# Attention scores: three single PSUM banks in a ring in place of pairs, with one exponential for each bank

## The reference, cut to what matters

```python
qkv = xf @ w_qkv + b_qkv                       # q, k, v: (b, heads, t, 32), t = 1024
scores = jnp.einsum('bhqd,bhkd->bhqk', q, k) * 32 ** -0.5
attn = jax.nn.softmax(scores, axis=-1)
o = jnp.einsum('bhqk,bhkd->bhqd', attn, v)     # then a projection and the residual
```

## Time and profile before

| | us |
|---|---|
| median of 3 runs | 5707.2 (5702.43 to 5717.48) |
| the profiled execution | 5702.98 |
| its span | 5701.3 |

### The profile page before, as it was taken

The page is one execution under the profiler, slowest core; times in us unless marked ns, Lnnn a source line. Parts: engine busy times, 40 slices in busy tenths (PEclk is TensorE's granted clock), DMA queues, the critical chain, the costliest instruction groups (busy, mean ns, idle before and its releaser), DMA issues.

```text
span 5701.3 us, 44537 instructions
## 1 busy us (share of the span) xinstructions
PE 4237.7 (74%) x16298; PEld 1839.3 (32%) x16298; DVE 3892.5 (68%) x4825; ACT 2109.0 (37%) x2575; POOL 2221.3 (39%) x721
## 2 busy tenths in 40 slices
PE   4678866788658886588865878658786587855878
PEld 2233422333224332243322433223332243322433
DVE  7764788647886478764787646876468774686746
ACT  3233442334423344233442435324253242542424
POOL 4541435414454044540445404444045440454404
PEclk7689977899778997699977999769897798976999
DMA  0020100211002100021000220002200012000120
GB/s 34 0 52 16 30 8 4 49 24 22 8 8 45 33 13 8 8 45 36 10 8 8 45 45 1 8 9 44 45 1 8 18 35 45 8 1 18 27 45 8
DMA packets 58845, 125.24 MB, mean 22 GB/s; under 512 B 14713, under 2 KB 16889, under 8 KB 58370
## 3 DMA queue, kind: packets, MB, share of 16 engines
q1 hardware_dynamic: 58626, 122.39, 9.2%
HBM read 12.23 MB, written 8.39 MB: 4 GB/s over the span
## 4 chain that ended last, share of the span: by engine, by line
PE 44%; DVE 34%; issue 9%; ACT 5%; SPq 4%; POOL 2%; DMA 2%; DVEq 0%; ACTq 0%; POOLq 0%
DVE mx L947 10%; PE PS L1288 8%; PE PS L1246 7%; PE PS L1080 6%; PE PS L1336 6%; PE PS L1370 4%; DVE work L839 3%; PE PS L1139 2%; DVE work L841 2%; PE PS L1180 2%; DVE mboth L954 2%; SPq L284 2%; PE PS L1297 2%; DVE small L714 2%; SPq L293 1%
## 5 line engine op out<-in xcount | busy, mean ns | idle before, releaser
L947 DVE TENSOR_REDUCE mx<-PS 128x1 f32<-128x512 f32 x2048 | 1336.3, 686 | 419.5 <-PE PS L1246 415.2
L617 ACT ACTIVATE PT<-PS 128x1024 f32<-128x1024 f32 x1024 | 1007.4, 1022 | 706.5 <-PE PS L1336 679.1
L1246 PE MATMUL PS<-KS,QS 96*128 96x512 f32 x2048 | 894.7, 479 | 194.6 <-DMA KS<-piece 84.6
L423 POOL TENSOR_TENSOR piece<-PT 128x2048 f32<-128x2048 f32 x48 | 219.9, 4581 | 2000.2 <-ACT PT L617 2000.2
L423 POOL TENSOR_TENSOR piece<-piece,PT 128x2048 f32<-128x2048 f32 x192 | 877.4, 4570 | 61.7 <-ACT PT L617 50.4
L399 POOL TENSOR_TENSOR work<-work,Crep 128x1024 f32<-128x1024 f32 x256 | 615.7, 2406 | 434.2 <-DVE work L839 240.9
L1336 PE MATMUL PS<-QS,KS 98*128 98x512 f32 x2048 | 685.2, 427 | 50.3 <-DMA QS<-nm 32.2
L1246 PEld LDWEIGHTS PS<-KS,QS 96*128 96x128 f32 x2048 | 376.7, 197 | 814.9 <-DVE mx L947 575.1
L1288 PE MATMUL PS<-PT,Vt 128*32 128x512 f32 x4096 | 554.1, 613 | 7.6 <-ACT PT L617 7.6
L1180 PE MATMUL PS<-dstk,sel 128*128 128x512 f32 (+1 forms) x640 | 313.1, 564 | 320.6 <-DVE work L841 133.5
L1180 PE MATMUL PS<-ustk,sel 128*128 128x512 f32 (+1 forms) x640 | 329.4, 587 | 285.4 <-DVE work L824 155.0
(11 more groups left out here) (212 smaller groups left out, 5556.3 us busy)
## 6 DMA issues: line engine op xcount, KB each, us to landing
QS<-piece SPq DMA_DIRECT2D x384, 128.0 KB, 2.4
KS<-piece SPq DMA_DIRECT2D x384, 128.0 KB, 2.4
xin<-x SPq DMA_DIRECT2D x8, 1024.0 KB
out<-xr SPq DMA_DIRECT2D x8, 1024.0 KB, 4.0
W<-wpack SPq DMA_DIRECT2D x2, 1024.0 KB
QS<-nm SPq DMA_DIRECT2D x128, 8.0 KB, 1.9
W<-wpack SPq DMA_DIRECT2D x1, 576.0 KB
W<-wpack SPq DMA_DIRECT2D x2, 256.0 KB
```

The costliest lines, as they stand in the source:

```text
L423: pool.tensor_tensor(total, first, PT[:, i % 3, :, :], ALU.add).then_inc(sum_pool.sem, 1)
L617: act.activation(PT[:, i % 3, 2 * pr:2 * pr + 2, :], PS[:, 2 + 2 * pr:4 + 2 * pr, :], ACT.Exp, scale=SCALE).then_inc(p_sb.sem, 1)
L947: dve.tensor_reduce(mx[:, cc, at:at + 1], PS[:, row_slot(n, cc), :], AX.X, ALU.max).then_inc(r_max.sem, 1)
L1246: pe.matmul(PS[:, row_slot(n, cc), :], QS[0:kd, c, h, q * P:q * P + P], KS[0:kd, h, cc * N:cc * N + N], start=True, stop=True).then_inc(r_ ...
```

## The change

The scores of the four heads go in turn through banks 2, 3 and 4 (`score_slot`), and each bank has an exponential of its own over 512 columns: twice as many (2048 in place of 1024), of half the width. A score waits for the exponential three scores earlier. The row scores go in turn through banks 5, 6 and 7, and one waits for the maximum three row scores earlier; in the prologue nothing changes but how the same wait is written. The second row score of a step is issued behind score 2 in place of behind score 3. Semaphore counts follow (`p_sb` and `s_ps` count single scores; the values, POOL's and DVE's additions wait for all four of a step, as before). The transpose of the turn still goes to bank 6.

```diff
@@ -53,6 +53,7 @@
 TURN_AT = 7
 AHEAD = 3
 NORM_AT = 4
+RING = 3
 PHASE_ROWS = sum(HALF_ROWS) // NC
 
 POOL_SUMS = (0, 1, 2, 3, 5, 6)
@@ -238,7 +239,7 @@
         nm_in = sig("nm_in", 2 * PHASES * 2 * 16)
         sum_pool = sig("sum_pool", 2 * (PHASES - 1) * (len(POOL_SUMS) - 1))
         sum_dve = sig("sum_dve", 2 * (len(DVE_SUMS) - 1))
-        s_ps, p_sb = sig("s_ps", 128), sig("p_sb", 128)
+        s_ps, p_sb = sig("s_ps", 256), sig("p_sb", 256)
         pv_ps, den_ln, den_rc = sig("pv_ps", 64), sig("den_ln", 8), sig("den_rc", 8)
         o_raw, o_sb = sig("o_raw", 8), sig("o_sb", 8)
 
@@ -419,7 +420,7 @@
                             first = PT[:, key_step(a, ph, 0) % 3, :, :] if k == 1 else total
                             if k > 1:
                                 pool.wait_ge(*sum_pool(b, pool_sums(a, ph, k - 1)))
-                            pool.wait_ge(*p_sb(b, 2 * i + 2))
+                            pool.wait_ge(*p_sb(b, GH * i + GH))
                             pool.tensor_tensor(total, first, PT[:, i % 3, :, :], ALU.add).then_inc(sum_pool.sem, 1)
                 pool.wait_ge(*x_new(b, 16))
 
@@ -612,9 +613,9 @@
                             done = summed(a, *divmod(i % (PHASES * KT) - 3, KT))
                             if done:
                                 act.wait_ge(*(sum_pool, sum_dve)[done[0]](b, done[1]))
-                        for pr in range(2):
-                            act.wait_ge(*s_ps(b, 2 * i + pr + 1))
-                            act.activation(PT[:, i % 3, 2 * pr:2 * pr + 2, :], PS[:, 2 + 2 * pr:4 + 2 * pr, :],
+                        for j in range(GH):
+                            act.wait_ge(*s_ps(b, GH * i + j + 1))
+                            act.activation(PT[:, i % 3, j, :], PS[:, score_slot(i % (PHASES * KT), j), :],
                                            ACT.Exp, scale=SCALE).then_inc(p_sb.sem, 1)
                         if kt == TURN_AT and ph < PHASES - 1:
                             neg_max(ph + 1)
@@ -995,7 +996,7 @@
                     first = PT[:, key_step(a, ph, 0) % 3, :, :] if k == 1 else total
                     if k > 1:
                         dve.wait_ge(*sum_dve(b, dve_sums(a, k - 1)))
-                    dve.wait_ge(*p_sb(b, 2 * i + 2))
+                    dve.wait_ge(*p_sb(b, GH * i + GH))
                     dve.tensor_tensor(total, first, PT[:, i % 3, :, :], ALU.add).then_inc(sum_dve.sem, 1)
                 normalize(ph)
 
@@ -1240,9 +1241,9 @@
                     if c == 0 and q == 0 and cc == 0:
                         pe.wait_ge(*stackedq[g][j](b, (a + 1) * 48))
                         pe.wait_ge(*stackedk[g][j](b, (a + 1) * 48))
-                    ahead = 2 if ph == 0 else 1
-                    if n % PHASE_ROWS >= ahead:
-                        pe.wait_ge(*r_max(b, halves(a, n - ahead, cc) + 1))
+                    ahead = 2 * NC if ph == 0 else RING
+                    if NC * (n % PHASE_ROWS) + cc >= ahead:
+                        pe.wait_ge(*r_max(b, halves(a, n, cc) - ahead + 1))
                     pe.matmul(PS[:, row_slot(n, cc), :], QS[0:kd, c, h, q * P:q * P + P], KS[0:kd, h, cc * N:cc * N + N],
                               start=True, stop=True).then_inc(r_ps.sem, 1)
 
@@ -1280,7 +1281,7 @@
                     g = ph // NC
                     sums = POOL_SUMS if ph < PHASES - 1 else DVE_SUMS
                     direct = [k for k in range(KT) if k not in sums]
-                    pe.wait_ge(*p_sb(b, 2 * i + 2))
+                    pe.wait_ge(*p_sb(b, GH * i + GH))
                     if kt == 0 and ph > 0:
                         pe.wait_ge(*o_raw(b, i // KT))
                     for j in range(GH):
@@ -1328,15 +1329,13 @@
                             else:
                                 next_rows(NC)
                             pe.wait_ge(*nm_in(b, 32 * (PHASES * a + ph + 1)))
-                        for pr in range(2):
-                            if ph + kt > 0:
-                                pe.wait_ge(*p_sb(b, 2 * i - 2 + pr + 1))
-                            for jj in range(2):
-                                h = GH * g + 2 * pr + jj
-                                ins = pe.matmul(PS[:, 2 + 2 * pr + jj, :], KS[:, h, kt * P:kt * P + P], QS[:, c, h, :],
-                                                start=True, stop=True)
-                            ins.then_inc(s_ps.sem, 1)
-                            next_rows(1)
+                        for j in range(GH):
+                            if GH * (KT * ph + kt) + j >= RING:
+                                pe.wait_ge(*p_sb(b, GH * i + j - RING + 1))
+                            pe.matmul(PS[:, score_slot(i % (PHASES * KT), j), :], KS[:, GH * g + j, kt * P:kt * P + P],
+                                      QS[:, c, GH * g + j, :], start=True, stop=True).then_inc(s_ps.sem, 1)
+                            if j in (1, 2):
+                                next_rows(1)
                         if kt > 0:
                             values(i - 1, next_rows, ph + 1 if kt == TURN_AT and ph < PHASES - 1 else None)
                         next_rows(row[1])
@@ -1402,7 +1401,12 @@
 
 def row_slot(n, cc):
 
-    return (4 + 2 * (n % 2) if n < PHASE_ROWS else 6) + cc
+    return 4 + 2 * (n % 2) + cc if n < PHASE_ROWS else 5 + (NC * (n % PHASE_ROWS) + cc) % RING
+
+
+def score_slot(i, j):
+
+    return 2 + (GH * i + j) % RING
 
 
 def halves(a, n, cc):
```

## The result

| | us |
|---|---|
| before, median of 5 runs | 5707.20 (5700.89 to 5717.95) |
| after, median of 5 runs | 5730.98 (5724.78 to 5735.08) |
| ratio after / before | 1.0037, 95% interval 1.002 to 1.0054 |
| the profiled execution of after, and its span | 5724.78, 5723.0 |

The changed kernel is slower by 24 us between the medians, and by 5723.0 - 5701.3 = 21.7 us between the two profiled spans. The forecast was +63. In the profiled executions the mean granted clock fell from 0.848 to 0.842.

A forecast was written before the change was run, and what follows sets the result against it. It took POOL's chain of five additions, then the turn through `mboth`, transpose and scores, to set each phase's pace. Terms -50 + 12 - 3 + 48 + 56 = +63 us on 5702.98 gave 5766 us, range just under 5710 to 5830.

The forecast's parts named there:

- POOL's gap: The wait ahead of POOL's fourth addition goes as row scores over three banks bring steps sooner: -50 us.
- Eight single exponentials: ACT's eight take 4.24 us, not 3.85: +12 us in phases 1 and 2, -3 us in phase 0.
- Phase 3: Three score banks make a closed round in phase 3: 2.74 us a step against 2.25, +48 us.
- The turn and the clock: PE stands longer before the transpose, TensorE's clock falls: 1.4 us in 40 of 48 turns, +56 us.
- some 2: Sign at the turn: PE's wait for the transpose comes near 2 us, against 1.09 before.
- One sign: Sign at the turn: `mboth` takes over 3 us and ends with POOL's fifth addition.
- the clock holds: Rival: TensorE's clock does not fall at the turns, so no clock term: 5710 us, no change; chance 0.20.
- `mboth` done in 0.2 us would bring 5573: Rival at the turn: `mboth` slips in between two POOL additions, -178 us, total 5573 us; chance 0.06.

The follow-up runs named there:

- rows2b: The changed kernel with row scores over two banks (6 and 7) in place of three, scores still on three banks; 5766.47 us, ratio 1.0103 to the kernel before.
- singles4b: The changed kernel, single exponentials kept, with scores over four banks (2 to 5) and row scores over two (6 and 7); 5703.77 us, ratio 0.9992 to before.
- fill: The changed kernel with seven matmuls of unread results ahead of each turn's transpose; 5696.95 us, ratio 0.9975 to the kernel before.
- before_fill: The kernel before the change with four useless matmuls ahead of each transpose; 5709.01 us, ratio 1.0006 to the kernel before.
- fill3: The changed kernel with three useless matmuls ahead of each transpose; 5692.72 us, ratio 0.9985 to the kernel before.
- red_sixb: The changed kernel with `mboth` as a one-input reduction and six score banks in phase 3; 5558.43 us, ratio 0.9734 to the kernel before.
- six: The changed kernel with scores over six banks (2 to 7) in phase 3 in place of three; 5677.97 us, ratio 0.9944 to the kernel before.
- red_after: The changed kernel with `mboth` made by a reduction over one SBUF operand; 5632.11 us, ratio 0.9868 to the kernel before.
- red_before: The kernel before the change with `mboth` made by a reduction over one SBUF operand; 5674.22 us, ratio 0.9943 to the kernel before.

## Why the prediction was wrong in size

**POOL's gap: right.** -46.4 us measured against -50. rows2b, which differs from the changed kernel in the third row-score bank alone, shows that this bank did it; singles4b agrees.

**Eight single exponentials: forecast too dear.** The four of 1024 took 3.85 us; ACT's timeline at the start of phase 2 now has

```profile
1810.58 3.99 ACT L618 ACTIVATE PT<-PS 128x512 f32<-128x512 f32 x8
```

3.99, not the 4.24 I worked out. On the loop that is 0.14 us more, not 0.39. Neighbours overlap by (8 x 0.60 - 3.99) / 7 = 0.12, where I had carried over the 0.08 of the wider ones. With phase 0 it came to +1.4 against +9.

**Phase 3: the mechanism right, the baseline wrong.** The closed round was forecast at 2.74 us a step and takes 2.69; against an undisturbed phase 3 of before it costs (25.42 - 22.6) x 16 = 45 us, forecast 48. But the kernel before had not 16 undisturbed ones. Two of its phases 3 by windows:

```profile
453.40:476.00 22.60, 19.93 (x112) 6.70 (x112) 14.93 (x8) 17.56 (x20) 0.00 (x0) 1.00 0.00 1
698.50:722.70 24.20, 21.47 (x112) 7.08 (x112) 14.94 (x9) 17.69 (x20) 0.00 (x0) 0.93 0.00 1
```

Five of the 16 ran partly at the low level and took 24.16 to 25.68 us, together 12 us more; in the changed kernel none did. So the term, mean against mean, is +32. I had quoted such a stretch as a price for the clock and not asked how often the kernel before already paid it.

**The turn and the clock: the mechanism right, the count wrong.** This is the step that failed most: "1.4 us in 40 of 48 turns". `mboth` still ended with POOL's fifth addition, PE stood 1.81 us for the transpose (forecast "some 2"), the clock fell behind it, and fill, with before_fill as its control, shows that the low clock cost the 34 us. The price was right: 35.2 / 22 = 1.6 us a turn, forecast 1.4. I had said 40 of 48 turns, and it was 22: +35 in place of +56. The number 40 came from a single stretch, the prologue's end, as if every turn like it had to fall; but the spared turn above had the same 1.81 us of standing and held, and fill3 shows how little more work it takes for all 48 to hold. What picks the 22 out of 48 turns that look alike stays open.

One sign was not met: `mboth` took 2.72 us and not "over 3". The forecast's own numbers did not give 3 either: it was to be issued 20.6 us into the loop, and POOL's additions were to end at 23.2, which makes 2.6.

**The sum.** -46 + 1 + 32 + 35 = +22 in place of -50 + 9 + 48 + 56 = +63. Of the 41 us between them 21 are the count of turns, 16 phase 3 with its baseline, 8 the eight exponentials, less 4 for the gap. Of the rivals, *the clock holds* is what fill built: 5697 us, where I had 5710. Without the clock's term the measured terms add up to -46 + 1 + 32 = -13 where I had +7; on the median of 5707 that is 5694. The forecast that `mboth` done in 0.2 us would bring 5573 came from another way there (it would have slipped between two additions, which it did in none of the 48 turns: the shortest was 2.42 us), but the loop that it described is nearly red_sixb's, 30.8 us against 30.0.

**The rule on the clock.** In the turn of 1803.68 and before it PE was busy again and again, with the longest wait 1.81 us, and the clock fell. The Trainium skill ("TensorE: Matmul & The Clock Gate", Part 1) has it fall, in its table, after an idle stretch; by that rule alone the term would have been nothing, and the changed kernel would have come to some 5696 us. The runs decide against that reading: 22 turns fell, and filling them won 34 us.

**The rule on the ports.** `mboth` took 174 ns where POOL was idle, 2720 under its additions, and 187 as a reduction with one operand under the same additions. The Trainium skill ("SBUF — State Buffer", Who interferes with whom) names a VectorE operation with two SBUF inputs as one that needs the ports shared with GpSimd; the three numbers agree, and they show the way out, which is one input.

## What to carry to other kernels

When a change takes away a wait that lay under a longer chain, ask where PE will stand instead: here 0.7 us more of standing at one place switched TensorE to 1.2 GHz in 22 of 48 turns, for the very stretch in which PE was the path, and took back 35 us of a gain of 46. Before a clock term goes into a sum, count how often each stage of the old kernel already runs at the low level. And look at how a tiny operation on the path reads its operands: `mboth` with one input, together with six banks where no row scores need them, turned a change of +0.4% into one of -2.7%.

## What was not expected of the hardware

Three useless matmuls, 0.96 us on PE from first to last, were enough to keep all 48 turns at 2.4 GHz, as well as seven did. More work on the engine made the kernel faster: by 38 us between the medians (5730.98 and 5692.72), and by some 30 us if each is compared with the kernel before as timed beside it (ratios 1.0037 and 0.9985).

A low clock moves. six changed nothing in the turns, and 33 fell in place of 22; red_after had none in the turns and 12 in its phases 3; the changed kernel had none in phase 3 where the one before had five. The time outside the phases moved too, in stages that no edit touched: 3705.7 us before and 3705.0 in the changed kernel, but 3726.3 in red_before, 3724.6 in red_sixb and 3694.2 in fill3. Each of these figures is of one execution, and executions of one kernel differ too: the twelve of fill3 took 5684.91 to 5716.38 us, at a mean granted clock of 0.84 to 0.85, and the slowest two had the lowest clocks; six's profiled execution had 0.835 where its others had 0.839 to 0.841. So how much of such a difference belongs to the kernel and how much to the execution is not shown. For red_sixb it goes with the clock: from the end of a sample's first attention to the first scores of its second, TensorE was at the low level for 27.5 to 38.3 us in the eight samples (22.6 to 27.2 before), and the stretch took 122.9 to 126.1 us (121.1 to 124.0). Why the low level came more often there was not tried.
